# A vision transformer tower on one core: token weights in chunks, x rows and h rows stored under semaphores of their own

## The reference, cut to what matters

```python
# x: 64 images of 224 x 224 x 3; patches of 16 x 16, so 14 x 14 = 196 patches and a class token, D = 192
concat = jnp.concatenate([images] + [_crop_shift_pad(images, oh, ow) for oh, ow in offsets], axis=-1)
h = patches(concat) @ W + b                       # token embedding, K = 16*16*15 = 3840
h = concatenate([cls_tok, h], axis=1)             # 64 x 197 x 192
h = h + attn(layernorm(h))                        # 12 heads of 64, 4-bit fake quantisation throughout
h = h + ffn(layernorm(h))                         # ternary weights, 8-bit activations, hidden 512
```

## Time and profile before

| | us |
|---|---|
| median of 3 runs (lowest, highest) | 1308.37 (1306.78, 1312.17) |
| the profiled execution | 1312.79 |
| its span, first to last instruction | 1310.6 |
| PE busy in the span | 1129.8 (86%) |
| DVE busy | 1084.5 (83%) |
| ACT busy | 937.1 (71%) |
| POOL busy | 475.0 (36%) |

### The profile page before, as it was taken

How to read it: one execution, slowest core, us unless ns; L and a number is a source line. 1 busy time by engine, 2 the same in 40 slices (tenths; PEclk the granted TensorE clock), 3 DMA queues, 4 the chain that set the end, 5 groups by cost and what they waited for, 6 DMA issues and landing times.

```text
span 1310.6 us, 31925 instructions
## 1 busy us (share of the span) xinstructions
PE 1129.8 (86%) x10782; PEld 696.3 (53%) x10782; DVE 1084.5 (83%) x1978; ACT 937.1 (71%) x1877; POOL 475.0 (36%) x540
## 2 busy tenths in 40 slices
PE   4999996599999999999999999998457677767776
PEld 4999995145555555555555555554334344434443
DVE  4566778179999999999999999999478888989995
ACT  0000000599999999999999999997168888888886
POOL 7444444002222222222222222222256666666664
PEclk9999998799999999999999999999557876777776
DMA  6999995136555556555555566555312322332322
GB/s 242 297 286 292 288 302 178 43 123 148 146 150 147 141 139 137 137 148 147 150 145 141 138 137 140 146 145 147 68 50 80 88 85 80 88 90 84 89 69 76
DMA packets 157637, 187.62 MB, mean 143 GB/s; under 512 B 42784, under 2 KB 119664, under 8 KB 157168
## 3 DMA queue, kind: packets, MB, share of 16 engines
q1 hardware_dynamic: 86352, 136.71, 32.7%
q10 hardware_dynamic: 55808, 39.65, 9.9%
q0 software_dynamic: 15360, 9.70, 8.5%
HBM read 143.06 MB, written 36.12 MB: 137 GB/s over the span
## 4 chain that ended last, share of the span: by engine, by line
PE 70%; ACT 8%; DVE 6%; issue 6%; ACTq 4%; DMA 3%; POOL 2%; SPq 0%; DVEq 0%; POOLq 0%
PE psum L1088 18%; PE psum L1148 11%; PE psum L1031 11%; PE psum L1135 8%; PE psum L1118 7%; PE psum L1179 6%; PE psum L1101 5%; ACT yi L579 2%; ACTq L449 2%; DMA big<-xt 2%; ACT big L572 2%; ACT ysq L599 2%; DVE big L1006 1%; ACT zi L587 1%; PE psum L1200 1%
## 5 line engine op out<-in xcount | busy, mean ns | idle before, releaser
L674 POOL DMA_DIRECT2D h_res<-att x128 | 143.4, 1169 | 574.3 <-ACT att L517 565.2
L883 DVE TENSOR_TENSOR pi<-big 128x2364 int16<-128x2364 f32 (+1 forms) x128 | 334.7, 2615 | 3.4 <-DMA big<-z_row 3.2
L541 ACT ACTIVATE big<-psum 128x788 f32<-128x788 f32 (+1 forms) x384 | 317.0, 828 | 1.2 <-DVE pi L883 1.2
L1031 PE MATMUL psum<-big 128*128 128x192 f32 (+1 forms) x1200 | 196.8, 329 | 18.4 <-DMA big<-xt 18.4
L1031 PEld LDWEIGHTS psum<-big 128*128 128x128 f32 (+1 forms) x1200 | 194.8, 190 | 19.5 <-DVE big L719 17.0
L1088 PE MATMUL psum<-xT,w1b 128*128 128x394 bf16 x768 | 163.9, 337 | 27.4 <-DMA xT<-x_int 25.2
L1179 PE MATMUL psum<-winb,zT 96*128 96x512 bf16 (+1 forms) x396 | 151.1, 551 | 33.2 <-DVE big L1006 32.3
L503 ACT ACTIVATE qki<-psum 128x394 int16<-128x394 f32 x384 | 172.3, 512 | 4.8 <-PE psum L1088 3.8
L503 ACT ACT_TABLE_LOAD x1 | 1.3, 1283 | 239.7 <-issue 239.7
L1148 PE MATMUL psum<-big,sa_hot 128*32 128x197 f32 (+1 forms) x3072 | 168.2, 336 | 0.0
L708 POOL TENSOR_TENSOR big<-big,goutb 128x512 f32<-128x512 f32 (+1 forms) x99 | 123.7, 1270 | 81.6 <-DVE big L1006 81.6
(11 more groups left out here) (100 smaller groups left out, 1699.5 us busy)
## 6 DMA issues: line engine op xcount, KB each, us to landing
big<-z_row SPq DMA_DIRECT2D x192, 394.0 KB, 5.0
big<-xt SPq DMA_DIRECT2D x98, 384.0 KB, 4.4
tin<-h_res SPq DMA_DIRECT2D x49, 192.0 KB, 2.4
tres<-h_res ACTq DMA_DIRECT2D x49, 192.0 KB, 2.5
out<-oo ACTq DMA_DIRECT2D x49, 192.0 KB, 2.6
h_res<-big ACTq DMA_DIRECT2D x96, 96.0 KB, 3.8
x_int<-big ACTq DMA_DIRECT2D x96, 64.0 KB, 3.8
h_res<-att POOLq DMA_DIRECT2D x64, 96.0 KB, 3.4
```

Of the source, the lines that this page charges most:

```text
L541: act.activation(ex[0:r, tri, t, 4 * g:4 * g + 4, :].rearrange("p (a h) n -> p a h n", a=2), psum[0:r, 2 * t:2 * t + 2, 0:2 * N] .rearrang ...
L674: pool.dma_start(h_res[bass.ds(b - 4, 1), t0:t0 + r, :].rearrange("a n d -> (a n) d"), att[0:r, par, t, :], accum_op=ALU.add).then_inc(s_a ...
L883: v.tensor_tensor(pi[0:r, t, :, 0:N], ex[0:r, it, t, :, :], zb[0:r, ip, :, :], ALU.mult).then_inc(s_pi, 1)
L1031: last = mm(psum[p0:p0 + r, s, 0:D], xring[:, s, c * 128 + p0:c * 128 + p0 + r], weight_of(cls, c), start=(c == 0), stop=(c == KC - 1))
```

## The change

The raw weights are loaded as six chunks, alternating with the six tiles of the first pack, each with its own semaphore. VectorE sums the five copies of a chunk in one reduction as it comes. TensorE takes the first pack by diagonals: chunk c of tile s in step c + s.

The semaphore of the row stores is split: `s_h1` and `s_x1`. GpSimd waits for the h rows, VectorE for the x rows. From pack 13 on (LATE) ScalarE stores x rows only; SyncE stores h rows of packs 13 and 14 behind its last load, half the x rows of pack 15, two of the corners' x rows, and, after four transposing loads, in step 0, the h rows of pack 15, the corners and the class. The first transposing load waits for `s_x1` alone; `s_h1` is awaited in step 1 by SyncE and in step 4 by GpSimd.

On VectorE the scale of w_out is made where it was, but w_out is quantised behind the last x rows, and the statistics of the corner tiles come ahead of pack 15's x rows. TensorE no longer waits for `woutb` ahead of stage 2, but ahead of stage 3. ScalarE waits for `stage` to be free before stage 2.

```diff
-        STORED = [PACK * LAST * 16 + 16 * 10, PACK * LAST * 16]
+        STORED = [PACK * LAST * 8 + 16 * 5, PACK * LAST * 8]
...
+        LATE = LAST - 3
...
-            sp.dma_start(wraw[:, :, :, :], w_tok).then_inc(s_wraw, 16)
+            for c in range(KC):
+                sp.dma_start(wraw[:, c, :, :], w_tok[:, c, :, :]).then_inc(s_wraw[c], 16)
+                sp.dma_start(xring[:, c, :], xt[c:c + 1, :, :].rearrange("a p n -> p (a n)")).then_inc(s_x[c], 16)
...
-            load_pack(0)
...
+            def store_h(i):
+                sp.wait_ge(s_hp, i + 1)
+                for s in range(PACK):
+                    sp.dma_start(tile_rows(h_res, i, s), hp[:, i % 2, s, :]).then_inc(s_h1[i % 2], 16)
+
+            for i in range(LATE, LAST - 1):
+                store_h(i)
+            sp.wait_ge(s_xb, LAST)
+            for s in range(PACK // 2, PACK):
+                sp.dma_start(tile_rows(x_rows, LAST - 1, s), xb[:, 1, s, :]).then_inc(s_x1[1], 16)
+            sp.wait_ge(s_xb, LAST + 2)
+            for rows, dst in list(corner_rows(x_rows))[0:2]:
+                sp.dma_start(dst, xb[rows[0]:rows[1], 0, rows[2], :]).then_inc(s_x1[0], 16)
 
             for p in range(2):
-                sp.wait_ge(s_st1[p], STORED[p])
+                sp.wait_ge(s_x1[p], STORED[p])
...
             def image_step(b, par, tri):
+                if b == 0:
+                    store_h(LAST - 1)
+                    sp.wait_ge(s_hp, LAST + 2)
+                    for rows, dst in corner_rows(h_res):
+                        sp.dma_start(dst, hp[rows[0]:rows[1], 0, rows[2], :]).then_inc(s_h1[0], 16)
+                if b == 1:
+                    for p in range(2):
+                        sp.wait_ge(s_h1[p], STORED[p])
...
+            def store_pack(i, par, with_h, tiles=PACK):
                 act.wait_ge(s_xb, i + 1)
+                if with_h:
+                    act.wait_ge(s_hp, i + 1)
+                for s in range(tiles):
+                    act.dma_start(tile_rows(x_rows, i, s), xb[:, par, s, :]).then_inc(s_x1[par], 16)
+                    if with_h:
+                        act.dma_start(tile_rows(h_res, i, s), hp[:, par, s, :]).then_inc(s_h1[par], 16)
...
+                store_pack(i, i % 2, i < LATE, PACK if i < LAST - 1 else PACK // 2)
...
-            for k in range(1, 5):
-                v.tensor_tensor(weff[:, 0, :, :], wraw[:, :, 0, :] if k == 1 else weff[:, 0, :, :],
-                                wraw[:, :, k, :], ALU.add).then_inc(s_weff0, 1)
-                dve.wait_ge(s_weff0, k)
+            for c in range(KC):
+                dve.wait_ge(s_wraw[c], 16)
+                v.tensor_reduce(weff[:, 0, c, :], wraw[:, c, :, :].rearrange("p k d -> p d k"), AX.X, ALU.add)\
+                    .then_inc(s_weff0, 1)
...
-            quantise(LAST - 1, 1, LAST - 1, 0, PACK, 128)
             for s in range(2):
                 slot_stats(K + 1 + s, s, 0, 128, K + s)
...
+            quantise(LAST - 1, 1, LAST - 1, 0, PACK, 128)
+            dve.wait_ge(s_xb, LAST)
             quantise(LAST, 0, LAST, 2, 3, B)
             quantise(LAST, 0, LAST + 1, 0, 2, 128)
+            quantise_weight(3, 128, 4 * D, woutb[:, :, :].rearrange("p c n -> p (c n)"), wsc[:, 1:2], -1.0, 1.0)
+            dve.wait_ge(s_wq, 4)
...
-            pe.wait_ge(s_weff0, 4)
-            pack(0, INSIDE)
+            for d in range(PACK + KC - 1):
+                for s in range(PACK):
+                    c = d - s
+                    if 0 <= c < KC:
+                        pe.wait_ge(s_weff0, c + 1)
+                        pe.wait_ge(s_x[s], 16)
+                        last = mm(psum[:, s, 0:D], xring[:, s, c * 128:(c + 1) * 128], weight_of(INSIDE, c),
+                                  start=(c == 0), stop=(c == KC - 1))
+                        if c == KC - 1:
+                            last.then_inc(s_emb, 1)
...
-            pe.wait_ge(s_wq, 4)
+            pe.wait_ge(s_wq, 2)
+            pe.wait_ge(s_wsc, 3)
...
+            pe.wait_ge(s_wq, 4)
             over_pairs(pe, pair_step)
```

More of the change, by code:

```diff
@@ L134, in vit_tower_kernel @@
             (nc.sync.engine, nc.vector.engine, nc.gpsimd.engine))}
-        s_wraw = sem("wraw_loaded")
+        s_wraw = [sem(f"wraw_loaded_{c}") for c in range(KC)]
         s_bias = sem("biases_loaded")
@@ L155, in vit_tower_kernel @@
         s_hp = sem("h_plus_bias_ready")
-        s_st1 = [sem(f"stage1_stored_{p}") for p in range(2)]
+        s_h1 = [sem(f"h_stored_{p}") for p in range(2)]
+        s_x1 = [sem(f"x_stored_{p}") for p in range(2)]
         s_xpad = sem("x_rows_padded")
@@ L371, in dst_rows, with tile_rows, corner_rows @@
             return img[:, t0:t0 + 3 * GRID + 1:GRID, :]
+        LATE = LAST - 3
+        def tile_rows(dram, i, s):
+            g, half = s // 2, s % 2
+            if not isinstance(i, int) or i < P_IN:
+                return dst_rows(dram, i + 1, 1 + 4 * g, half, True)
+            y, x, along_x = [(0, 1, True), (GRID - 1, 1, True), (1, 0, False), (1, GRID - 1, False)][i - P_IN]
+            return dst_rows(dram, y, x + 4 * g, half, True) if along_x else dst_rows(dram, y + 4 * g, x, half, False)
+        def corner_rows(dram):
+            for c, (y, x) in enumerate([(0, 0), (0, GRID - 1), (GRID - 1, 0), (GRID - 1, GRID - 1)]):
+                p0 = (c % 2) * B
+                yield (p0, p0 + B, c // 2), dram[:, 1 + y * GRID + x, :]
+            yield (0, B, 2), dram[:, 0, :]
         @block.sync
         def _(sp):
-            sp.dma_start(wraw[:, :, :, :], w_tok).then_inc(s_wraw, 16)
+            for c in range(KC):
+                sp.dma_start(wraw[:, c, :, :], w_tok[:, c, :, :]).then_inc(s_wraw[c], 16)
+                sp.dma_start(xring[:, c, :], xt[c:c + 1, :, :].rearrange("a p n -> p (a n)")).then_inc(s_x[c], 16)
             sp.dma_start(sc[:, :], quant.partition_broadcast(128)).then_inc(s_quant, 16)
@@ L476, in _ @@
                     load_weight((0, 1, 3).index(i - PEEL) + 1)
-                border = [(0, 1, True), (GRID - 1, 1, True), (1, 0, False), (1, GRID - 1, False)]
-                store_pack(i, i % 2, *((i + 1, 1, True) if i < P_IN else border[i - P_IN]))
+                store_pack(i, i % 2, i < LATE, PACK if i < LAST - 1 else PACK // 2)
             act.wait_ge(s_xb, LAST + 2)
[L480 to L486, removed]
+            for rows, dst in list(corner_rows(x_rows))[2:]:
+                act.dma_start(dst, xb[rows[0]:rows[1], 0, rows[2], :]).then_inc(s_x1[0], 16)
             def added(image, par):
@@ L547, in image_step @@
                         n += 1
+            act.wait_ge(s_stage_free, 4)
             over_images(act, image_step)
@@ L670, in image_step @@
             def image_step(b, par, tri):
+                if b == 4:
+                    for p in range(2):
+                        pool.wait_ge(s_h1[p], STORED[p])
                 if has_unit(b, -4 * U1):
@@ L818, in ternary_sum, with ternary_scale @@
                                 apply_absolute_value=True).then_inc(s_wsum, 1)
-            def ternary_weight(n, k, rows, cols, dst):
+            def ternary_scale(k, rows, cols):
                 dve.wait_ge(s_wmean, k + 1)
```

33 lines of the change are left out of this document (11 added, 22 removed).

## The result

| | before | changed |
|---|---|---|
| median of 4 runs, us | 1308.26 | 1293.98 |
| lowest, highest | 1306.78, 1312.17 | 1292.61, 1294.73 |
| the profiled execution | 1312.79 | 1294.41 |
| its span | 1310.6 | 1292.4 |
| last stage-1 matmul ends (profile) | 217.40 | 209.96 |

The ratio is 0.9885 with a 95% interval of 0.9862 to 0.9908: 14.3 us faster by the medians, 1.1%, with the interval at 12.0 to 18.1 us. The time is inside the range of the prediction (1285 to 1299) and 4 us above its 1290.

The account below looks back on a forecast made before the run. TensorE was taken to bound stage 1, leaving only its idle time at both ends to gain: 7.2 us at the start plus 10.8 at the end, 18.0 off the 1308.4 median, gives 1290.4, entered as 1290; range 1285 to 1299.

Parts of the forecast that it names:

- The start: Start of stage 1: chunked token weights let pack 2 begin at 37.4 us instead of 44.57, gaining 7.2 us (4 to 9).
- The reduce: VectorE's sum of one weight chunk at the start: 1.1 us each, only the last exposed, weights complete at 16.6 us.
- slow first matmuls: TensorE's first pack: 528 ns matmuls instead of 326, partly hidden in waits for chunks; 1.0 us entered of 0 to 2.8.
- The stall beside w1: TensorE's wait for the x tile issued beside the w1 load: 0 to 1.5 us, 1.0 entered.
- The middle: Stage 1 from pack 2 until 186 us: TensorE is the bound and moves left unchanged, 0 us.
- The gap: TensorE's idle time between stage 1 and the first projection: first projection at 231.65 us, 10.8 us entered (7.1 to 11.5).
- the class copy: VectorE's copy of class rows at the end of stage 1: 0.24 us; what follows 2.1 later if it meets GpSimd's add.
- 3.3 us off the path: End of stage 1: quantising w_out moves behind the last x rows, taking 3.3 us off VectorE's path.
- the queue leaves the path: End of stage 1: store queues no longer bound; some 14 us of idle remain, with VectorE's last rows late next.
- (c): Start: strided reduce over 2.3 us makes all six count; no difference at 4.4 us (chance 0.05), slower from 5.3 (0.03).
- (b): Start gives only 0 to 3 us because constants and x tiles hold pack 1: 1295 to 1298 us, chance 0.10.
- (d): End of stage 1: transposing loads still end up behind h rows; 10.5 us gained, 1298 us, chance 0.02.

## Why the prediction was right, point by point

- **The start, 7.2 us: measured 7.4** (217.40 - 209.96), but the sum is right by luck, with two terms off in opposite ways. The reduce was taken at 1.1 us from contiguous rows and takes 1.78; weights are complete at 17.4, not 16.6. Against it, 1.0 us was set for slow first matmuls behind that point, and none are left: 21 products in 7.09 us are 0.338 each. The 528 ns matmuls all fall into the time of waiting for chunks. Pack 1 begins at 24.37 (24.7 predicted). The stall beside w1 was 1.00 as entered, but in other executions it is 0 to 2.1, so that the two agree is luck too. The last constants landed 10.7 us after 9.29, at 20.0 instead of 22.2, and were no bound.
- **The middle, 0: right**; 50.00 of 50 us busy. But "TensorE is the bound" until 186 us passes over the wait for w_in at its end (1.84 us before, 1.71 changed). It is a place where 0 to 2.5 us are lost, and with the slow clock 5.4.
- **The gap, 10.8 us: measured 9.2.** The step that was off is the class copy at 0.24 us, entered as if it came ahead of GpSimd's add. The add began 0.05 us before it, since its wait for the stores (0.45 us in the earlier trace rows) had gone with the split semaphores, and the copy took 2.67. The prediction had this case among its bounds, 2.1 us later, a sum of 8.9; it happened. The term "3.3 us off the path" for w_out was mis-sized: it is 0.8 to 1.0 us, because most of the 3.3 was waiting for the add, which passed to the instruction put in its place. The clips of pack 15 met a second add (1.61 us for 0.87), a term I had not; against it the corner rows, entered at 1.32 us beside that add, took 0.66 without it.
- **That the queue leaves the path: right.** Some 14 us were to remain, and VectorE to be late next; 16.1 remain and it is. The last x row landed in 1.95 us. The 11 h stores in step 0 were hidden: four transposing loads, the stores until 234.3, the fifth load at 236.96, after a wait for TensorE.
- **Not seen: the table load**, 0.9 us from the projection to the scores (10.84 against 9.97). A wait added in front of stage 2 on ScalarE moved a load that had been hidden. The prediction asked who is queued behind each added wait on SyncE and GpSimd, but not on ScalarE.
- **The sum**: 7.4 + 9.2 - 0.9 = 15.7 us, as the rows of the first scores say (252.61 and 236.86), against 18.0 entered and 14.3 (later 14.7) by medians. So 2.3 of the 3.7 us between forecast and median are explained, the gap's 1.6 and the table load above all; the other 1.4 lie within the interval of the measured gain (12.0 to 18.1) and the spread behind stage 1, and stay open. That the two profiled spans differ by 18.2, close to the 18.0, comes from 2.5 us of that spread in stages 2 and 3 and is no confirmation.
- **The rivals**: (c) by the mechanism true (the stride does cost), but at 1.8 us far from 2.3, where all six reduces would count. (b) and (d) didn't happen: pack 1 began at 24.37, and SyncE's list has no wait for h rows.

## What to carry to other kernels

- An instruction's length beside another engine's work is not its cost: ask whether it is waiting in that row, and who will wait there when it is moved. Here the cure was to move what it waited for, an add that nothing on the path needed.
- When a stall of a few us is left as it is, look at several executions: its size is a distribution (0 to 2.1 us beside w1 and 0 to 2.5 at w_in here), and in the two executions with the longest ones, 2.08 and 2.49 us, the clock fell as well.
- A wait added ahead of the first activation can land on the table load and uncover it; put it in front of earlier work of that queue.

## What the runs showed of the hardware

- TensorE idle for 2.49 us in the midst of a long busy stretch: granted clock down from 1.00 to 0.50, and 2.9 us lost over the next two packs. Idle for 2.08 us in another execution: 0.50 from about 47.5 to 51 us. After 0 to 1.84 us at such places it stayed at 1.00 in all other executions.
- In the gap of 13.4 to 25.6 us between the stages the clock fell to 0.50 in all twelve executions, and it was back at 1.00 only 3.0 to 9.0 us after the first projection.
- A VectorE copy, scaling or clip between SBUF operands took 2.65 to 2.98 us beside a GpSimd add of 2.61 to 2.67 us, instead of 0.24 to 0.62, also when it began 0.05 us after the add; statistics and adds from PSUM beside it keep their 0.35 us.
- A reduce of 960 f32 per partition: 1.15 us with neighbours read, 1.78 with one f32 every 768 bytes.
- A 384 KB load issued beside one of 2304 KB on the other queue took 9.4 to 11.5 us to land in eleven executions, about as long as the large one (9.5 to 11.8); beside pieces of 768 KB at most 7.0.
